# RK4 recurrence: the linear seed is written into PSUM by VectorE instead of added by TensorE

## What is computed

```python
def _derivative(q, p, drive, coupling, bias):
    i_couple = jnp.tanh(q) @ coupling.T
    dq = q - q ** 3 / 3.0 - p + drive + i_couple + bias
    dp = EPSILON * (q + ALPHA - BETA * p)
    return (dq, dp)
...
q_next = q + DT / 6.0 * (dq1 + 2 * dq2 + 2 * dq3 + dq4)
q_next = jnp.clip(q_next, -CLAMP, CLAMP)
```

## Time and profile before

| | us |
|---|---|
| median of three runs | 900.66 |
| lowest and highest of them | 899.45 and 900.99 |
| the profiled execution | 901.75 |
| its span (first to last instruction) | 900.0 |
| mean granted TensorE clock, as a share of full speed | 0.998 |

### The profile page before, as it was taken

How to read it: one execution, slowest core, us unless ns; L and a number is a source line. 1 busy time by engine, 2 the same in 40 slices (tenths; PEclk the granted TensorE clock), 3 DMA queues, 4 the chain that set the end, 5 groups by cost and what they waited for, 6 DMA issues and landing times.

```text
span 900.0 us, 18595 instructions
## 1 busy us (share of the span) xinstructions
PE 890.4 (99%) x7222; PEld 768.2 (85%) x7222; DVE 598.9 (67%) x1703; ACT 413.8 (46%) x1147; POOL 293.3 (33%) x382
## 2 busy tenths in 40 slices
PE   9999999999999999999999999999999899999998
PEld 8787888888888888888888878899987599999998
DVE  5554554655556545655576775777777888888887
ACT  3233322333223432234355664555545766666665
POOL 1654510112101201023623516333223555554343
PEclk9999999999999999999999999999999999999999
DMA  7313000000000000110004000000000000000000
GB/s 274 95 60 94 25 1 1 2 1 1 2 1 2 1 1 2 48 48 1 1 12 187 1 0 1 1 1 1 1 2 1 1 1 25 2 24 2 25 2 25
DMA packets 5705, 22.02 MB, mean 24 GB/s; under 512 B 880, under 2 KB 1264, under 8 KB 5232
## 3 DMA queue, kind: packets, MB, share of 16 engines
q1 hardware_dynamic: 5616, 20.82, 6.6%
HBM read 18.72 MB, written 2.10 MB: 23 GB/s over the span
## 4 chain that ended last, share of the span: by engine, by line
PE 94%; DVE 4%; ACT 1%; issue 1%; POOL 0%; DVEq 0%; ACTq 0%
PE ps L373 47%; PE ps L793 8%; PE ps L797 7%; PE ps L653 7%; PE ps L474 6%; PE ps L792 5%; PE ps L643 3%; PE ps L655 3%; PE ps L463 2%; PE ps L504 1%; PE ps L380 1%; DVE yt L1685 0%; PE ps L659 0%; DVE BD L1273 0%; DVE frs L1287 0%
## 5 line engine op out<-in xcount | busy, mean ns | idle before, releaser
L1232 DVE TENSOR_SCALAR qk<-ps,vec 128x512 f32<-128x512 f32 x64 | 48.1, 751 | 97.7 <-PE ps L373 97.7
L373 PE MATMUL ps<-x_hi,W_hi 128*128 128x512 f32 x256 | 102.1, 399 | 1.8 <-DVE V L1239 1.4
L890 ACT ACTIVATE qk<-ps,vec 128x512 f32<-128x512 f32 x64 | 44.1, 690 | 127.0 <-PE ps L373 127.0
L373 PE MATMUL ps<-x_lo,W_hi 128*128 128x512 f32 x256 | 99.9, 390 | 0.0
L373 PE MATMUL ps<-x_hi,W_lo 128*128 128x512 f32 x256 | 99.8, 390 | 0.0
L793 PE MATMUL ps<-rk_th,cpc 128*128 128x128 f32 x516 | 99.0, 294 | 0.1
L1243 DVE SCALAR_TENSOR_TENSOR o_lo<-ps,vec,o_hi 128x512 fp32r<-128x512 f32 x64 | 47.1, 744 | 71.6 <-ACT o_hi L906 68.2
L906 ACT ACTIVATE o_hi<-ps,vec 128x512 fp32r<-128x512 f32 x64 | 44.0, 687 | 108.3 <-PE ps L474 108.3
L793 PEld LDWEIGHTS ps<-rk_th,cpc 128*128 128x128 f32 x516 | 72.7, 191 | 9.1 <-ACT rk_th L1174 6.0
L792 PE MATMUL ps<-rk_th,cpc 128*128 128x64 f32 x508 | 77.8, 255 | 0.0
L653 PE MATMUL ps<-ht,hh 128*128 128x128 f32 x512 | 77.1, 283 | 0.1
(11 more groups left out here) (302 smaller groups left out, 2147.1 us busy)
## 6 DMA issues: line engine op xcount, KB each, us to landing
stage<-qkv_w SPq DMA_DIRECT2D x6, 768.0 KB, 4.3
stage<-out_w SPq DMA_DIRECT2D x4, 512.0 KB, 3.8
f_raw<-ffn_w SPq DMA_DIRECT2D x2, 1024.0 KB, 5.0
xorig<-xT SPq DMA_DIRECT2D x1, 2048.0 KB, 8.5
x_all<-xT SPq DMA_DIRECT2D x1, 1536.0 KB, 14.7
out<-xtb SPq DMA_DIRECT2D x3, 512.0 KB, 3.1
ada_sb<-ada_w SPq DMA_DIRECT2D x1, 1024.0 KB, 9.6
BD<-qkv_w SPq DMA_DIRECT2D x1, 768.0 KB, 6.1
```

Of the source, the lines that this page charges most:

```text
L373: r = pe.matmul(out_, lhsT, rhs, start=first and i == 0, stop=last and i == n - 1)
L890: act.activation(qk[:, 0, h % 2, :], ps[:, PJ[0], :], ACT.Identity, bias=col("qkv_b", HU * u + h)).then_inc(act_evac, 1)
L1232: dve.tensor_scalar(qk[:, 1, h % 2, :], ps[:, PJ[1], :], col("qkv_b", HEADS + HU * u + h), None, ALU.add).then_inc(dve_evac, 1)
```

## The change

Four things change in the RK4 loop. DVE writes `E1`, `Z2`, `Z3` and `Z4` straight into the PSUM banks in which the coupling adds up (`seed`), and all the `linear` passes go, but for the one of step 0. In their place PE has idle passes: 2 + 2 after evaluations 2 and 4, 5 + 2 after 1 and 3, with the wait for the seed (`seeded`) ahead of the last two. On DVE, `w1` and `w2` move ahead of `Z2` and `Z3`, `w4` ahead of `P`, and `qa` ahead of `E1`. And `mine` is asked for ahead of `coupling`.

```diff
-RK_DVE = ("q", "U2", "Z2", "w1", "q2a", "q2b",
-          "t3", "s1", "Z3", "w2", "q3a", "q3b",
+RK_DVE = ("q", "U2", "w1", "Z2", "q2a", "q2b",
+          "t3", "s1", "w2", "Z3", "q3a", "q3b",
           "s2", "Z4", "s3", "w3", "q4a", "q4b",
-          "s4", "P", "w4", "E1", "qa", "qb")
+          "s4", "w4", "P", "qa", "E1", "qb")
...
             def tanh_done(t, k, half):
                 pe.wait_ge(rk_act, RK_ACT_START + at(t, RK_ACT, f"th{k}{half}"))
+
+            def seeded(t, k):
+                step, name = (t - 1, "E1") if k == 1 else (t, f"Z{k}")
+                pe.wait_ge(rk_dve, RK_START + at(step, RK_DVE, name))
...
                 coupled(k, 0, 1, False, True).then_inc(rk_pe, 1)
                 coupled(k, 1, 0, False, False)
                 coupled(k, 1, 1, False, True).then_inc(rk_pe, 1)
+                keep_warm(2)
+                if k == 2:
+                    seeded(t, 3)
+                elif t < T - 1:
+                    seeded(t + 1, 1)
+                keep_warm(2)
 
             def chunks_together(t, k):
                 tanh_done(t, k, "a")
@@ -814,6 +824,9 @@
                 tanh_done(t, k, "b")
                 coupled(k, 0, 1, False, True).then_inc(rk_pe, 1)
                 coupled(k, 1, 1, False, True).then_inc(rk_pe, 1)
+                keep_warm(5)
+                seeded(t, k + 1)
+                keep_warm(2)
...
             for t in range(T):
                 if t:
-                    pe.wait_ge(rk_dve, RK_START + at(t - 1, RK_DVE, "E1"))
-                    linear(1, "E1")
                     chunks_together(t, 1)
                 else:
                     first_evaluation()
-                pe.wait_ge(rk_dve, RK_START + at(t, RK_DVE, "Z2"))
-                linear(2, "Z2")
-                if t == 0:
+                    seeded(0, 2)
+                    linear(2, "Z2")
                     keep_warm(WARM_START)
                 chunks_in_turn(t, 2)
-                pe.wait_ge(rk_dve, RK_START + at(t, RK_DVE, "Z3"))
-                linear(3, "Z3")
                 chunks_together(t, 3)
-                pe.wait_ge(rk_dve, RK_START + at(t, RK_DVE, "Z4"))
-                linear(4, "Z4")
                 chunks_in_turn(t, 4)
...
+            def seed(k):
+                lo = RK_BANK[k % 2][0]
+                return ps[:, lo:lo + KC, 0:B]
...
                 inc(STT(r_["U2"], r_["P"], -K2, r_[f"D{t % 3}"], M, Ad))
-                mine("U2")
-                inc(STT(r_["Z2"], r_["q"], 1 - A_ * C_, r_["U2"], M, Ad))
                 if t:
                     act_done("sq1")
                 else:
                     dve.wait_ge(rk_first, 1 + RK_FIRST.index("sq1"))
+                mine("q")
                 inc(STT(r_["w"], r_["qsq" if t else "w4"], -(C_ + 1), r_["q"], Ad, M))
+                mine("U2")
+                inc(STT(seed(2) if t else r_["Z2"], r_["q"], 1 - A_ * C_, r_["U2"], M, Ad))
+                mine("w1")
                 a1 = coupling(1, 0)
-                mine("w1")
                 inc(dve.tensor_tensor(half("q2", 0), a1, half("w", 0), Su))
...
+                act_done("sq2")
+                mine("q2b")
+                inc(STT(r_["w"], r_["qsq"], -C_, r_["q2"], Ad, M))
                 mine("t3")
-                inc(STT(r_["Z3"], r_["q2"], -A_ * C_, r_["t3"], M, Ad))
-                act_done("sq2")
-                inc(STT(r_["w"], r_["qsq"], -C_, r_["q2"], Ad, M))
+                inc(STT(seed(3), r_["q2"], -A_ * C_, r_["t3"], M, Ad))
+                mine("w2")
                 a2 = coupling(2, 0)
-                mine("w2")
                 inc(dve.tensor_tensor(half("q3", 0), a2, half("w", 0), Su))
...
                 mine("q3b")
-                inc(STT(r_["Z4"], r_["q3"], 2 * (1 - A_ * C_), r_["b4"], M, Ad))
+                inc(STT(seed(4), r_["q3"], 2 * (1 - A_ * C_), r_["b4"], M, Ad))
...
+                mine("w3")
                 a3 = coupling(3, 0)
-                mine("w3")
...
                 mine("q4b")
                 if t < T - 1:
                     inc(STT(r_["s4"], r_["q4"], W4, r_["s3"], M, Ad))
-                    mine("s4")
-                    inc(dve.tensor_scalar(r_["P"], r_["s4"], C_ * (CLAMP - SHIFT), C_ * (-CLAMP - SHIFT), ALU.min, ALU.max))
                 act_done("sq4")
                 inc(STT(r_["w4"], r_["qsq"], -(C_ + 1) / 3, r_["q4"], Ad, M))
                 if t == T - 1:
                     break
+                mine("s4")
+                inc(dve.tensor_scalar(r_["P"], r_["s4"], C_ * (CLAMP - SHIFT), C_ * (-CLAMP - SHIFT), ALU.min, ALU.max))
+                mine("w4")
+                a4 = coupling(4, 0)
+                inc(STT(half("qraw", 0), a4, 1 / 3, half("w4", 0), M, Su))
                 mine("P")
-                inc(dve.tensor_tensor(r_["E1"], r_[f"D{(t + 1) % 3}"], r_["P"], Su))
-                a4 = coupling(4, 0)
-                mine("w4")
-                inc(STT(half("qraw", 0), a4, 1 / 3, half("w4", 0), M, Su))
+                inc(dve.tensor_tensor(seed(1), r_[f"D{(t + 1) % 3}"], r_["P"], Su))
                 inc(STT(half("qraw", 1), coupling(4, 1), 1 / 3, half("w4", 1), M, Su))
```

More of the change, by code:

```diff
@@ L791, in coupled @@
                 if last:
-                    return pe.matmul(ps[:, RK_BANK[k % 2][c], 0:B], w, th, start=first, stop=last)
-                return pe.matmul(ps[:, RK_BANK[k % 2][c], 0:2 * B], w, twice(th), start=first, stop=last)
+                    return pe.matmul(ps[:, RK_BANK[k % 2][c], 0:B], w, th, start=first, stop=last, skip_group_check=True)
+                return pe.matmul(ps[:, RK_BANK[k % 2][c], 0:2 * B], w, twice(th), start=first, stop=last, skip_group_check=True)
             def linear(k, z):
                 for c in range(KC):
-                    pe.matmul(ps[:, RK_BANK[k % 2][c], 0:2 * B], ident[:, :], twice(rk[z][:, c, :]), start=True, stop=False)
+                    pe.matmul(ps[:, RK_BANK[k % 2][c], 0:2 * B], ident[:, :], twice(rk[z][:, c, :]), start=True, stop=False, skip_group_check=True)
             def tanh_done(t, k, half):
                 pe.wait_ge(rk_act, RK_ACT_START + at(t, RK_ACT, f"th{k}{half}"))
+            def seeded(t, k):
+                step, name = (t - 1, "E1") if k == 1 else (t, f"Z{k}")
+                pe.wait_ge(rk_dve, RK_START + at(step, RK_DVE, name))
             def chunks_in_turn(t, k):
@@ L838, in first_evaluation @@
                 for c in range(KC):
-                    pe.matmul(ps[:, RK_BANK[1][c], 0:B], ident[:, :], rk["E1"][:, c, :], start=False, stop=True).then_inc(rk_pe, 1)
+                    pe.matmul(ps[:, RK_BANK[1][c], 0:B], ident[:, :], rk["E1"][:, c, :], start=False, stop=True, skip_group_check=True).then_inc(rk_pe, 1)
             for t in range(T):
                 if t:
-                    pe.wait_ge(rk_dve, RK_START + at(t - 1, RK_DVE, "E1"))
-                    linear(1, "E1")
                     chunks_together(t, 1)
```

## The result

| | median, us | runs | lowest and highest |
|---|---|---|---|
| before, on the same chip | 900.94 | 6 | 899.45 and 908.09 |
| after | 904.66 | 6 | 904.33 and 908.25 |

The ratio of after to before is 1.0046, 95% interval 1.0024 to 1.0068. The kernel became slower, by about 3.7 us, where 5.2 were forecast (905.9 us). The profiled execution took 904.61 us, its span 902.9. Five views of it answer to the rows of before.

What follows compares the result with a forecast made beforehand. The prediction took the ACT-PE-DVE ring, not PE, as the bound. Terms +0.16, -0.05, +0.07, -0.07 and +0.06 made +0.17 us a step, +5.2 us in all, giving 905.9 us, range 902.2 to 908.5.

Steps and rivals of the forecast that it cites:

- The ring: RK4 loop: tanh on ACT, coupling on PE, subtraction on DVE, four times; seven intervals sum to 5.87 us a step.
- `P` behind `w4`: Late `P` delays `V3`, `V5` and `th1a` on ACT; evaluation 1's first coupling load (S1) comes 0.16 us later.
- The separate wait: DVE's wait for PE becomes its own instruction: +0.07 us each at `q2a` (net -0.05) and `q3a`, +0.06 at `q4a`.
- `Z3` has 0.01 of room: DVE, evaluation 2: `Z3` ahead of `q3a` sets a floor of 0.75 us against PE's 0.76, so no added cost.
- the seeds' write costs nothing: DVE writing seeds into PSUM: the 0.02 us longer write is not on the ring, so nothing is counted.
- rival 1: DVE's separate wait costs nothing; +0.08 us a step, with +0.05 at `q3a` by `Z3`; 903.1 us, chance 0.13.
- S3 -0.07: Evaluation 3's first coupling load on PE comes 0.07 us earlier once the identity passes are gone.
- idle passes hidden: PE's seven (0.45 us) or four (0.25 us) idle passes fit before the next tanh and cost nothing.
- rival 2: Faster: `V5` isn't in the way of `th1a` and the separate wait is free; -0.14 us a step, 896.3 us, chance 0.12.
- rival 3: No change: `V5` isn't in the way, waits cost 0.20 us, offset by 0.12 and 0.07; 900.6 us, chance 0.05.
- `w1` leave the ring at `q2a`: DVE: `w1` ahead of `Z2` starts some 0.10 us earlier and no longer delays `q2a`; -0.12 us a step.
- the upper bound: `th1a` 0.22 us behind `V5` and a seed write costing 0.07 on the ring: 7.8 us slower, 908.5 us.

Runs made afterwards that it cites:

- e1: The kernel after the change with `P` put back ahead of `w4`; 906.14 us, ratio to before 1.0061.
- e3: The kernel after with `P` ahead of `w4` and the four pairs of waits in their old order; 904.81 us, ratio to before 1.0045.
- e4: The kernel before with only DVE's seeds in PSUM and TensorE's idle passes, DVE's order and waits unchanged; 900.27 us, ratio 1.0000.
- g1: The kernel after with TensorE's wait for the seed moved to the coupling, written behind the wait for the tanh; 903.74 us, ratio to before 1.0035.
- g2: The kernel after with TensorE's wait for the seed moved to the coupling, written ahead of the wait for the tanh; 909.02 us, ratio to before 1.0096.
- f1_v5_late: The kernel after with `V5` moved on ACT from ahead of the first tanh to behind `sq1`; 903.85 us, ratio to before 1.0041.
- g3_one_idle_pass: The kernel after with one idle pass behind each coupling instead of four or seven; 904.49 us, ratio to before 1.0050.
- f4_e1_ahead_own: The kernel after with `P` and `E1` in their old places and DVE's own wait separate as before; 897.26 us, ratio to before 0.9971.
- f3_p_first_u3_late: The kernel after with `P` ahead of `w4` and GpSimd's `U3` issued behind the store of the step; 899.56 us, ratio to before 0.9993.

## Why the prediction was right, point by point

- *The ring and the period before* (5.87): adding the seven intervals gives the step of every kernel in the table. What missed, in e1, e3, e4, g1 and g2, was an interval foreseen wrongly.
- *`P` behind `w4`, +0.16 at S1.* The mechanism is right: `V5` ahead of `th1a`, 0.20 apart as forecast, no idle time between them, and with `V5` out of the way S1 falls by 0.20 (f1_v5_late). This is the term of the sum that was mis-sized: +0.11 measured. `w4` began at 0.30 and not 0.32, `P` at 0.51 and not 0.53, `P` took 0.28 for 0.29, and `th1a` 0.24 for 0.26. Such hundredths in a row made 0.05 a step, 1.5 us, the whole distance between forecast and result. Against e4_seeds_alone, the price of the late `P` is 0.20, since the seeds alone bring S1 forward by 0.09; the prediction's 0.16 was the net of both.
- *The separate wait, +0.07 at `q3a`, +0.06 at `q4a`, -0.05 at `q2a`.* Measured +0.07, +0.06 and -0.05. e3_p_first_own against e1_p_first, which differ in the order of the waits alone, shows it again at `q3a` (0.77 to 0.70). The Trainium skill, "Perfetto Trace Analysis", section "Per-engine timelines", draws an instruction for the sequencer alone with its wait in the sequencer, and one for the engine with a wait queue of its own behind the sequencer; the trace agrees that the two cost differently (0.09 to 0.11 against 0.04 on DVE, 0.06 more on TensorE).
- *`Z3` has 0.01 of room, the seeds' write costs nothing.* Seeds into two PSUM banks took 0.28 to 0.29. Nothing was lost there. But the floor of 0.75 that the prediction gave `Z3` was too high: in e3_p_first_own `q3a` stands 0.70 behind S2 with `Z3` ahead of it, 0.19 behind the start of `Z3`, where after has 0.26. The room was nearer 0.06 than 0.01, and rival 1's +0.05 at `q3a` has no ground.
- *S3 -0.07, idle passes hidden.* Both measured so; g3_one_idle_pass shows the second directly.
- *Rival 1 (the separate wait is free)* falls by `q3a`, *rival 2 (faster)* by `V5` and `th1a`, *rival 3 (no change)* by the ratio. Rival 2 was nevertheless the nearest to a real possibility: f4_e1_ahead_own is the change without its late `P`, its late `E1` and its new order of waits, and it is faster (step 5.77, where rival 2 had 5.73).
- *Two side sums of the prediction are off.* Rival 3's +0.01 a step gives 901.0 and not 900.6; the upper bound, 0.165 + 0.02 + 0.07 a step, gives 8.0 us and not 7.8. The forecast doesn't use either.
- *Not seen:* `q` at 348 ns, held up by GpSimd's `U3`. The start of `U3` hangs on `V3` and so on `P`; whoever moves `P` moves a GpSimd instruction, and the prediction followed `P` only into ACT's queue. It has `w1` leave the ring at `q2a` and gives no room for it; the room was 0.02. That the longer `q` cost nothing in after was luck. The same collision decided f1, by `q`, and e1, by `E1`.

The account of a step, by the table. From before to e4_seeds_alone: S1 -0.09, `q2a` +0.09, S3 -0.07, `q4a` +0.07, nothing in sum. From there to after: S1 +0.20 (the late `P`), `q2a` -0.15 (the coupling comes later against `w1`, and `w1` stands ahead of `Z2`), `q3a` +0.07 (the separate wait), `q4a` -0.01: +0.12, to 5.98 with rounding. Against the best kernel, f4_e1_ahead_own, after loses 0.21 a step: 0.14 where `q2a` stands behind S4 (2.38 to 2.52), which is the late `P` by way of `V5`, and 0.07 at `q3a`, which is the separate wait. f3_p_first_u3_late, with `P` early and the new order of waits, has `q2a` at 2.38 too.

## What to carry to other kernels

When an instruction is moved in one engine's queue, follow its result into every queue that reads it, GpSimd's too, and ask which instruction it will then run beside. Work taken from TensorE pays only where TensorE's arrival was the last of the two events that the next engine waits for. Here DVE's own chain was level with it at `q4a` and behind it at `q2a`, so the seeds alone gave nothing; the gain came with a shorter chain on DVE. Where two waits stand ahead of one instruction, have the instruction carry the one that is released last, and check in the trace which of the two it does carry.

## What the hardware showed unexpectedly

- *DVE and GpSimd hold each other up where both read SBUF.* `q` (one SBUF tile in and out) took 348 ns beside `U3` and 227 without; `E1` (two SBUF tiles) 588 and 290; `t3` (two SBUF tiles) 506 and 290. `q` ended 0.08 behind the GpSimd instruction, the others about 0.15. `s1`, with one input in PSUM, began beside GpSimd's `m` and took 289 ns. In before `U3` and `q` only just missed each other: `U3` ended at 767.70 and `q`, of 0.23, began at 767.68 (timeline of before, GpSimd, then DVE):

```profile
767.24 0.46 POOL L2070 TENSOR_TENSOR rk_U<-rk_D,rk_V 128x128 f32<-128x128 f32 x1 [1.15 <-ACT rk_V L1151]
```

```profile
767.68 0.23 DVE L1731 TENSOR_SCALAR rk_q<-rk_qraw 128x128 f32<-128x128 f32 x1
```

  The Trainium skill, "SBUF — State Buffer", section "Who interferes with whom", says that a DVE instruction with two SBUF inputs contends with a GpSimd instruction that reads SBUF, that a `tensor_scalar` in a 2-port mode does too, and that whichever starts first blocks the other. The rows agree that the later one is held, with one addition: if it did all its work behind the other, `E1` would end 0.29 behind `U3`; it ended 0.15 behind. GpSimd is held too: its `m`, which takes 456 ns in after, took 506 in f3_p_first_u3_late, where it begins while the held `t3` still runs (by line and form, GpSimd, of that run):

```profile
L2079 POOL TENSOR_TENSOR rk_m<-rk_q,rk_q 128x128 f32<-128x128 f32 x31 | 15.7, 506 | 0.0
```

  Not every overlap costs. In after `U2`, with two SBUF tiles as inputs, begins 0.16 ahead of GpSimd's addition into `xtb`, and neither is longer for it (288 and 456 ns). Why that one goes free, no run shows.
- *The clock.* With one idle pass per coupling, and TensorE idle for 17% of the loop, the granted clock stayed 1.00.
